# The low part of probability unit 5 on VectorE, and unit 3's shift in front of x's low part, in a cross-attention and expert kernel

## The reference

```python
x = x + attention(layernorm(x), ctx, ctx)      # q = x w_q + b_q; scores / 4; softmax over 77 keys; w_o, b_o
h = layernorm(x)
probs = softmax(h @ router_w); top_w, top_i = top_k(probs, 2)
for e in range(8):
    out += cw[:, e] * ((silu(h @ gate_w[e]) * (h @ up_w[e])) @ down_w[e])
x = x + out
```

## Time and profile before

| | us |
|---|---|
| median of 3 runs | 911.65 (908.09 to 916.79) |
| the profiled execution | 910.35 |
| its span, first to last instruction | 908.5 |
| granted TensorE clock, mean | 0.985 |

### The profile page before, as it was taken

One profiled execution on the slowest core, in us unless ns is written; L12 is line 12 of the kernel. 1 busy time (PEld: TensorE's weight loads), 2 busy tenths in 40 slices (PEclk: granted clock), 3 DMA queues, 4 the chain that ended last, 5 costly groups with the idle time before them and its releaser, 6 DMA issues.

```text
span 908.5 us, 32045 instructions
## 1 busy us (share of the span) xinstructions
PE 843.3 (93%) x11936; PEld 770.9 (85%) x11936; DVE 588.6 (65%) x1757; ACT 479.8 (53%) x900; POOL 342.4 (38%) x637
## 2 busy tenths in 40 slices
PE   4889899899999987799999999999999999999995
PEld 3677777777777776699999999999999999999995
DVE  6789788788888756566466457446646648544442
ACT  5777777788887774444354335324424435333331
POOL 4789566655666555241122221222222122222112
PEclk9999999999999989899999999999999999999999
DMA  6211322222222543495355228225525632223221
GB/s 211 88 46 45 95 76 66 80 79 68 84 82 66 110 147 119 93 201 132 50 99 122 29 55 174 36 39 108 118 30 99 135 60 36 35 29 32 35 35 18
DMA packets 109876, 74.04 MB, mean 81 GB/s; under 512 B 66444, under 2 KB 99802, under 8 KB 109818
## 3 DMA queue, kind: packets, MB, share of 16 engines
q1 hardware_dynamic: 83898, 36.09, 16.9%
q0 software_dynamic: 13536, 19.85, 12.3%
q10 hardware_dynamic: 12384, 17.35, 7.5%
HBM read 36.27 MB, written 26.80 MB: 69 GB/s over the span
## 4 chain that ended last, share of the span: by engine, by line
PE 75%; issue 5%; ACT 4%; DVE 4%; POOL 1%; DMA 1%; another core or an unknown queue 1%; ACTq 0%; SPq 0%; DVEq 0%; POOLq 0%
PE bank L630 16%; PE bank L632 16%; PE bank L631 16%; PE bank L825 6%; PE bank L827 6%; PE bank L826 6%; PE bank L699 3%; PE bank L706 3%; ACT probs L938 1%; ACT pt_hi L944 1%; DMA raw_tail<-expert_rows 1%; DVE xt_lo L1155 1%; PE bank L755 1%; ACT xt_hi L925 1%
## 5 line engine op out<-in xcount | busy, mean ns | idle before, releaser
L630 PE MATMUL bank<-xg,e_hi 128*128 128x128 f16 x2176 | 374.6, 220 | 5.2 <-issue 3.4
L632 PE MATMUL bank<-xg,e_lo 128*128 128x128 f16 x2176 | 374.6, 220 | 0.5 <-issue 0.5
L631 PE MATMUL bank<-xg,e_hi 128*128 128x128 f16 x2176 | 374.6, 220 | 0.0
L1702 POOL DMA_INDIRECT out<-y_sb,tok_row x67 | 108.4, 1618 | 425.8 <-DVE y_sb L1456 404.2
L630 PEld LDWEIGHTS bank<-xg,e_hi 128*128 128x128 f16 x2176 | 214.0, 98 | 7.2 <-issue 3.1
L631 PEld LDWEIGHTS bank<-xg,e_hi 128*128 128x128 f16 x2176 | 214.0, 98 | 2.8 <-issue 1.2
L632 PEld LDWEIGHTS bank<-xg,e_lo 128*128 128x128 f16 x2176 | 214.0, 98 | 0.0
L1008 ACT ACTIVATE g_act<-bank 128x512 f32<-128x512 f32 x136 | 81.2, 597 | 223.0 <-PE bank L632 207.1
L1461 DVE SCALAR_TENSOR_TENSOR h_full<-bank,g_act 128x512 f32<-128x512 f32 x136 | 94.0, 691 | 121.7 <-ACT g_act L1008 120.7
L825 PE MATMUL bank<-e_hi,h_hi 128*128 128x256 f16 x544 | 148.9, 274 | 4.5 <-DVE h_lo L1467 3.1
L827 PE MATMUL bank<-e_hi,h_lo 128*128 128x256 f16 x544 | 148.8, 274 | 0.9 <-issue 0.8
(11 more groups left out here) (193 smaller groups left out, 1685.8 us busy)
## 6 DMA issues: line engine op xcount, KB each, us to landing
e_stage<-in_gate_w ACTq DMA_DIRECT2D x24, 256.0 KB
e_stage<-in_up_w ACTq DMA_DIRECT2D x22, 256.0 KB
e_stage<-in_down_w ACTq DMA_DIRECT2D x20, 256.0 KB
expert_rows<-pads SPq DMA_DIRECT2D x8, 530.0 KB
xin<-in_x SPq DMA_DIRECT2D x16, 256.0 KB, 3.0
xres<-in_x SPq DMA_DIRECT2D x16, 256.0 KB
out<-x SPq DMA_DIRECT2D x16, 256.0 KB
k_diag<-k_parts SPq DMA_DIRECT2D x124, 9.6 KB
```

What stands on the lines that cost most here:

```text
L630: pe.matmul(dst, a_hi(c), b_hi(c), start=c == 0, stop=False)
L631: pe.matmul(dst, a_hi(c), b_lo(c), start=False, stop=False)
L632: mm = pe.matmul(dst, a_lo(c), b_hi(c), start=False, stop=ends and c == chunks - 1)
L1702: pool.indirect_dma_start(out, bass.IndirectOffsetOnAxis(tok_from[:], 0), y_from[:], None, compute_op=ALU.add).then_inc(added, 16)
```

## The change

Two edits. Unit 5 leaves `LOW_ON_ACT`: TensorE's `take_high` and ScalarE's `low_probs` of unit 5 fall away in unit 6 of each body, and VectorE's `low_probs` of unit 5 comes in there, behind the shift of unit 7, with one more call of `between`. The counts that `low_done` waits for follow (6 and 2 a batch rather than 7 and 1). And `low_x` moves from `inner` to `outer` of unit 2, so that VectorE's order there is maximum of unit 3, shift of unit 3, `low_x`, `low_att` rather than maximum, `low_x`, shift, `low_att`.

```diff
--- before.py
+++ after.py
@@ -50,7 +50,7 @@
 RSQRT_SEED = 0x5F3759DF
 LN_STEPS = 2 + 12 + 2
 SHORT = 2
-LOW_ON_ACT = (0, 1, 2, 3, 4, 5, 6)
+LOW_ON_ACT = (0, 1, 2, 3, 4, 6)
 ROUTE = 3
 STAGES = 6
 SCATTER = NT * 16
@@ -1349,12 +1349,11 @@
                 slots_chain = take_slots(z, z.plus % 2) if z else None
 
 
-                inner = {2: [(a, low_x)],
-                         3: [(n, lambda j: sum_x(j, 0, xin, x_in, 16, x_summed)),
+                inner = {3: [(n, lambda j: sum_x(j, 0, xin, x_in, 16, x_summed)),
                              (r, lambda j: high_rows(j, rows_at(j)))]}
                 outer = {0: [(a, full_kv)],
                          1: [(c, lambda j: normalize(j, 1))],
-                         2: [(c, low_att)],
+                         2: [(a, low_x), (c, low_att)],
                          4: [(c, residual), (a, lambda j: low_q(j, j.plus % 2))],
                          5: [(b, lambda j: normalize(j, 0)), (c, lambda j: sum_x(j, 1, x2, x2_ready, 1, x2_summed)),
                              (m, lambda j: gather(j, n, c) if by_pool(n, b) else start(statistics(j, n, c)))],
```

## The result

| | before | after |
|---|---|---|
| median | 910.92 (908.09 to 916.79) | 922.03 (920.27 to 923.32) |
| ratio, with its 95% interval | | 1.0105 (1.0072 to 1.0138) |
| profiled execution, span | 910.35, 908.5 | 922.88, 921.1 |
| its granted TensorE clock, mean | 0.985 | 0.974 |
| first matmul of the expert stage | 332.27 | 345.34 |

A forecast was written before the change was run, and what follows sets the result against it. A loop through several engines, with GpSimd's scatters in it, was taken to set attention's 19.5 us bodies. 910.35 + 1.5 (early bodies) - 2.5 (hold) = 909.35; the median lies 1.3 higher, so 910.5 us, range 904 to 917.

The forecast's parts named there:

- The take-off of unit 5 gone, its gain a wait on unit 7's shift: TensorE, unit 6: 0.25 us of matmul and 0.32 idle go, but become a wait on VectorE's shift of unit 7.
- ScalarE's copy gone, 0.25 us sooner through units 7, 0 and 1: ScalarE loses one 0.593 us copy a batch; TensorE and ScalarE run 0.25 us earlier down to unit 1's transposes.
- 0.6 us more on VectorE, covered by the 1.87 us before xt_lo: VectorE's added subtraction takes 0.6 us of queue a batch; in steady bodies its 1.87 us wait before xt_lo covers it.
- The shift of unit 3 ahead of x's low part costs nothing: VectorE, before xt_lo: the 0.47 us shift fits the wait; first two scatters about 0.3 earlier, gaining nearly nothing alone.
- The hold on unit 1's transposes partly gone, 2.5 us: Transposes told before the fourth scatter: 0 to 0.50 us saved a body, 0.25 taken, 2.5 us in ten bodies.
- rival A: Unit 1's completions stay late or others are caught; steady bodies keep 19.5 us, early loss remains: 913 us, chance 0.25.
- Early bodies, 1.5 us: First three batches, without scatters, bound by VectorE from unit 5 to unit 1: 0.9 to 1.8 us lost, 1.5 taken.
- The sum: Whole kernel: 910.35 + 1.5 - 2.5 = 909.35 for the profiled execution; median 1.3 above it, so 910.5 predicted.
- rival B: VectorE becomes the bound in all bodies, sixteen times 0.6, 9.6 us slower: 921 us, chance 0.08.
- sentences on what would prove me wrong in kind: Signs in the profile after; the last: a wait that no case names, such as one on unit 5's low part.

The follow-up runs named there:

- e1: Only unit 5's low part moved to VectorE, x's low part left ahead of unit 3's shift, on the kernel before: 910.5 us, ratio 0.9996 to it.
- e5: The kernel before, neither edit, plus a spare GpSimd cast and its wait ahead of the first pair of scatters: 926.5 us, ratio 1.0102 to the kernel before.
- e6: Only unit 5 on VectorE, plus a spare GpSimd cast and its wait ahead of the first scatter pair: 901.2 us, ratio 0.9828 to the kernel before.
- e4: The changed kernel plus a spare GpSimd cast and its wait ahead of the first pair of scatters: 898.9 us, ratio 0.9855 to the kernel before.
- e2: Only unit 3's shift moved ahead of x's low part, unit 5 as in the kernel before: 919.8 us, ratio 1.0084 to the kernel before.
- e13: The changed kernel with GpSimd's split of v moved ahead of the first scatter pair, no added work: 902.1 us, ratio 0.9816 to the kernel before.
- e14: The kernel before, neither edit, with GpSimd's split of v moved ahead of the first scatter pair: 925.9 us, ratio 1.0076 to the kernel before.
- e7: The changed kernel plus a spare GpSimd subtraction, its end not waited for, ahead of the first scatter pair: 915.2 us, ratio 0.9988 to the kernel before.
- e12: Only the move of unit 3's shift, plus a spare GpSimd cast and wait ahead of the first scatter pair: 926.2 us, ratio 1.0101 to the kernel before.
- e9: The changed kernel plus two plain GpSimd DMAs at the first scatter pair's old place and a spare cast: 919.0 us, ratio 1.0032 to the kernel before.

## Why the prediction was wrong

1. *The take-off of unit 5 gone, its gain a wait on unit 7's shift.* Right in kind, and with unit 5 alone in size: that wait is 6.4 us in eleven bodies in e1, 0.58 each, what was taken away (0.57). With both edits it is 11.5 us in eleven, 1.02 in the body shown, since the shift itself is late (below).
2. *ScalarE's copy gone, 0.25 us sooner through units 7, 0 and 1.* Shown by e1 (unit 1's transposes 0.25 to 0.40 us sooner), and in its effect by e5 and e6: with it the pt_hi that waited for no recorded releaser goes from ten times to one, and the last pair holds nothing of note in e4 and e6.
3. *0.6 us more on VectorE, covered by the 1.87 us before xt_lo.* Right. The cover fell to 12.8 us in eleven bodies in e1 and no body of it took longer for that.
4. *The shift of unit 3 ahead of x's low part costs nothing, and makes the first two scatters 0.3 sooner, "nearly nothing".* **This is the step that failed.** Its sizes were right: the shift of unit 3 starts at 229.94 and ends before xt_lo at 230.71, and the scatters are 0.37 us sooner. But the step priced that only by whether the scatters were the last to come in the loop, "so this alone gives nearly nothing"; alone it cost 0.84% in e2, some 8 us. The scatters are also a cause of held completions, as the same prediction had read from the fourth. Before, unit 3's value product began its last matmul 0.06 or 0.23 us after the first scatter's start and its end got through; now it is 0.43 or 0.62 after, and its end is held, for 0.6 or 1.1 us. After 0.6 the body mostly still takes 19.7 us. After 1.1 TensorE stands idle, in all four such bodies of the ten the clock then falls for 3.4 us, TensorE's late work meets the last pair, and the body takes 21.4 to 22.0 (in e2 one such body keeps its clock and takes 20.5). Ten bodies lose 10.3, of which about 8 at the lower clock by the estimate above.
5. *The hold on unit 1's transposes partly gone, 2.5 us.* Right for unit 5 alone, where the profiled ten bodies gained 5.8, more than the 0 to 5.0 of the bounds; wrong for the whole change, where the hold on another completion outweighed it. The prediction named this ("it may catch other completions, at unit 4 or 5") but gave it no price: its bounds, 0 and 0.50 a body, were both gains, where the row of pt_hi behind the fourth scatter offered 0.87 idle a body as the loss. In the trace of the kernel before the last matmul of unit 3's product starts at 209.70, 0.23 us after a scatter's start at 209.47. Ten bodies by 0.87 are 8.7 us, and rival A's 913 with them is 922; that this meets the measured time is luck, as most of the real loss passes at the lower clock.
6. *Early bodies, 1.5 us.* The profile has 3.1 us by the fourth recorded batch (86.13 for 83.06). But that stretch varies by itself: it is 84.50 in e1 and 87.11 in e6, whose programs are the same up to there. It goes with the clock: up to these marks 3.4 us (before), 10.2 (after and e1) and 13.6 (e6) pass at the lower one. So whether 1.5 is right wasn't settled.
7. *The sum.* It has no term for the granted clock, though the page of the kernel before gave its mean as 0.985; after it is 0.974. (Its own terms give 909.35 + 1.3 = 910.65, rounded to 910.5.)

Rival A (913) had the loss too small and the forecast had a gain; rival B's 921 is nearly the measured time for a reason that e4 and e13 refute. A number that fits isn't the mechanism, and B's is luck: B asked for waits on VectorE because VectorE is full, and there VectorE itself was idle, 12.4 us of it before the reciprocal. Of the sentences on what would prove me wrong in kind, the last applied: a wait appeared that no case named.

On the rule of the Trainium skill weighed there (SBUF — State Buffer, "SBUF: two separate sides"), the after profile again shows GpSimd's Newton steps at 0.20 us each (220.54 and 220.81) beside unit 5's subtraction on VectorE (220.29 for 0.68 us), so nothing hangs on it.

## What to carry to other kernels

In a loop in which GpSimd issues indirect DMAs, look at which completions of TensorE fall due around each issue before shifting the one against the other, even by a few tenths of a microsecond and in the direction that looks good, and price a loss there as well as a gain. An edit that only makes something earlier still moves what that something disturbs. Read the granted clock of each body before putting its length down to waits: here a body with one stretch of 3.4 us at half the clock was 1 to 2 us longer, and the waits in it looked like holds. Where a completion is told late without a releaser in the trace, try to put the issue somewhere else with necessary work: here that was worth more than both edits, but only together with unit 5 on VectorE: on the kernel before it cost 0.8% (e14).

## What the runs showed of the hardware

TensorE's completions reach the other engines late if they fall due while GpSimd issues a pair of indirect DMAs (each 128 rows; 1.03 and 0.98 us on GpSimd, 1.35 apart), while TensorE goes on. The readers start at a few places: some 0.3 to 0.75 us after the first one's start where the completion isn't held (before, e4, e7); 1.32 to 1.38 after it (after, e7); 0.7 to 0.84 (after) or 1.5 to 1.6 (before, e5) after the second one's. What was held is up to 1.9 us of idle time for its reader (e12). Two plain DMAs of the same size, issued by GpSimd in 1.21 us, held nothing (e9), so DMAs of that size and GpSimd's being busy with issuing them don't suffice.

The granted TensorE clock falls from 1.00 to 0.50 for 3.4 us at a time in single bodies (five of ten in after, four in e2). In it a take-off takes 0.64 us for 0.41, four transposes 1.06 for 0.60, and TensorE got through 28 matmuls where it did 54.

By the Trainium skill (Perfetto Trace Analysis, "DMA Instruction — SWDGE (GPSIMD)") the recorded time of a DMA from GpSimd is the making of its descriptors and not the movement of data. That agrees with a hold that goes with the 1.03 us records, but the plain ones are recorded the same way and held nothing. Which of its resources the completions wait for, no run here shows.
